# Layer 3 attention: TensorE's steps written out, two sets of key parts, value products in one piece

## The reference, cut to what matters

```python
q = q_input @ W_Q + b_Q                     # 16 x 56 x 128, as 16 heads of 8
k = kv_input @ W_K + b_K                    # 16 x 1500 x 128
v = kv_input @ W_V + b_V
sim = jnp.einsum('bhqd,bhkd->bhqk', q, k) / jnp.sqrt(jnp.float32(D_H))
sim = jnp.where(mask, neg_inf, sim)
attn = jax.nn.softmax(sim, axis=-1)
out = jnp.einsum('bhqk,bhkd->bhqd', attn, v)
...
return out @ W_O + b_O
```

## Time and profile before

| | us |
|---|---|
| Median of 3 runs | 1829.14 (1823.56 to 1829.15) |
| The profiled execution | 1828.54 |
| Its span | 1826.8 |
| PE busy in the span | 1546.7 (85%) |
| DVE busy | 1257.7 (69%) |
| ACT busy | 834.4 (46%) |
| POOL busy | 321.7 (18%) |

### The profile page before, as it was taken

How to read it: one execution, slowest core, us unless ns; L and a number is a source line. 1 busy time by engine, 2 the same in 40 slices (tenths; PEclk the granted TensorE clock), 3 DMA queues, 4 the chain that set the end, 5 groups by cost and what they waited for, 6 DMA issues and landing times. The chain is left out here.

```text
span 1826.8 us, 40229 instructions
## 1 busy us (share of the span) xinstructions
PE 1546.7 (85%) x15246; PEld 1295.7 (71%) x15246; DVE 1257.7 (69%) x2561; ACT 834.4 (46%) x1241; POOL 321.7 (18%) x437
## 2 busy tenths in 40 slices
PE   3897397456899999999999995679898889897895
PEld 2896276336799999999999982346676667675795
DVE  4313653685788888888888873367676768785698
ACT  1332132133566666666666640335454445453332
POOL 0110000001323343323343300030000000000230
PEclk8898698667999999999999998789999999999898
DMA  2112598000211111111111000153544354450210
GB/s 40 40 35 72 125 228 195 25 9 1 68 35 35 35 36 58 40 34 34 34 36 59 6 0 6 29 139 88 121 97 111 91 118 110 99 116 8 70 36 22
DMA packets 93087, 116.02 MB, mean 64 GB/s; under 512 B 12337, under 2 KB 78306, under 8 KB 92962
## 3 DMA queue, kind: packets, MB, share of 16 engines
q1 hardware_dynamic: 92962, 114.19, 24.8%
HBM read 76.35 MB, written 0.46 MB: 42 GB/s over the span
## 5 line engine op out<-in xcount | busy, mean ns | idle before, releaser
L2306 DVE TENSOR_REDUCE l3att_parts<-PS 112x1 f32<-112x500 f32 x384 | 244.3, 671 | 104.3 <-PE PS L2049 103.3
L1728 ACT CAST l2att_PT<-PS 125x512 fp32r<-125x512 f32 x336 | 175.2, 594 | 221.1 <-PE PS L1667 221.1
L1768 DVE TENSOR_REDUCE l2att_neg<-PS 128x1 f32<-128x1500 f32 x112 | 192.7, 1721 | 77.6 <-PE PS L1660 77.6
L1774 DVE TENSOR_TENSOR l2att_PT<-PS,l2att_PT 125x512 fp32r<-125x512 f32 x336 | 210.2, 681 | 1.5 <-ACT l2att_PT L1728 1.5
L2049 PE MATMUL PS<-l3att_KS,l3att_QB 97*112 97x500 f32 x384 | 169.0, 492 | 47.0 <-issue 24.2
L2180 ACT ACTIVATE l3att_P<-PS 125x1344 f32<-125x1344 f32 x128 | 165.3, 1291 | 77.4 <-PE PS L2068 77.4
L1667 PEld LDWEIGHTS PS<-all_ident,l_P 128*125 128x125 f32 x1344 | 163.5, 187 | 14.6 <-DVE l_P L1782 6.0
L1737 ACT ACTIVATE l_P<-PS,l2att_neg 128x1500 f32<-128x1500 f32 x112 | 171.2, 1529 | 5.0 <-DVE l2att_neg L1768 5.0
L1699 PE MATMUL PS<-l2att_PT,l_cc 125*128 125x256 f32 x576 | 170.5, 296 | 0.0
L1667 PE MATMUL PS<-all_ident,l_P 128*125 128x128 f32 x1344 | 165.4, 273 | 4.3 <-DVE l_P L1782 4.3
L1701 PE MATMUL PS<-l2att_PT,l_cc 125*128 125x256 f32 x576 | 162.5, 282 | 0.0
(11 more groups left out here) (518 smaller groups left out, 2960.1 us busy)
## 6 DMA issues: line engine op xcount, KB each, us to landing
l3att_KS<-l3att_kh SPq DMA_DIRECT2D x128, 187.5 KB, 4.3
l_QP<-in_ctxT SPq DMA_DIRECT2D x8, 1500.0 KB, 11.5
l_cT<-in_ctxT SPq DMA_DIRECT2D x16, 750.0 KB
l_c<-in_ctx SPq DMA_DIRECT2D x16, 750.0 KB
l3att_cT<-in_ctxT SPq DMA_DIRECT2D x16, 750.0 KB, 4.5
l3att_KS<-l3att_kl SPq DMA_DIRECT2D x64, 187.5 KB, 4.4
l_QP<-in_ctx SPq DMA_DIRECT2D x8, 1344.0 KB
l0f_w<-in_L_ffn_W SPq DMA_DIRECT2D x16, 256.0 KB, 3.1
```

What stands on the lines that cost most here:

```text
L1728: act.copy(PT[:, 4 * g:4 * g + 4, PLACE[u1], 0, :], PS[0:CHUNK, 3 * s1 + g, :].rearrange("k (c r) -> k c r", r=128)).then_inc(hi_in, 1)
L1768: v.tensor_reduce(neg[:, s:s + 1], E, XY_AXES, ALU.max, negate=True).then_inc(top_in, 1)
L1774: v.tensor_tensor(PT[:, 4 * g:4 * g + 4, at, 1, :], PS[0:CHUNK, 3 * s1 + g, :].rearrange("k (c r) -> k c r", r=128), PT[:, 4 * g:4 * g + 4 ...
L2306: v.tensor_reduce(parts[:, u % 2, half, i:i + 1], PS[0:HROWS, PLACES[p], 0:BANK_KEYS], X_AXIS, ALU.max, negate=True).then_inc(top_in, 1)
```

## The change

Three edits, all in `attend_sets`:

- PE's steps 0 to 68 are all written out; ACT, DVE and POOL keep their loops.
- `kh` and `kl` become two tiles each, taken in turn by the batch, and ACT's wait for the copies of the batch before is gone.
- In PE's step all 12 chunks of `values` come in one piece after `rows` 0 and 1, with a wait for both `powers` of step n-1. `rows` 2 moves behind the value projection, next to `rows` 3. Between `turned` 0 and `turned` 1 only `rows` 4 and 5 stay.

```diff
-            kh, kl = (self.sb(ctx, n, [128, KEYS], F32R) for n in ("kh", "kl"))
+            kh, kl = ([self.sb(ctx, f"{n}{s}", [128, KEYS], F32R) for s in range(2)] for n in ("kh", "kl"))
...
-                        for r, src, done in ((0, kh, kh_in), (1, kh, kh_in), (2, kl, kl_in)):
+                        for r, src, done in ((0, kh[s], kh_in), (1, kh[s], kh_in), (2, kl[s], kl_in)):
...
-                    def values(chunks):
+                    def values():
                         s, a = (u - 2) % UNROLL // SETS, (u - 2) % SETS
-                        if chunks[0] == 0:
-                            pe.wait_ge(m_in, n - 1)
-                            if known is None or known >= 4:
-                                pe.wait_ge(o_in, n - 3)
-                            pe.wait_ge(vh_in, (n - 2) // SETS * BANKS + BANKS)
-                            if known == 2:
-                                pe.wait_ge(blank, 1)
-                        for k in chunks:
-                            if k % PART == 0 or k == chunks[0]:
-                                pe.wait_ge(p_in, 2 * n - 3 + k // PART)
+                        pe.wait_ge(m_in, n - 1)
+                        if known is None or known >= 4:
+                            pe.wait_ge(o_in, n - 3)
+                        pe.wait_ge(vh_in, (n - 2) // SETS * BANKS + BANKS)
+                        pe.wait_ge(p_in, 2 * n - 2)
+                        if known == 2:
+                            pe.wait_ge(blank, 1)
+                        for k in range(CHUNKS):
...
                     if before:
-                        values((0, 1, 2, 3))
+                        values()
                     if then:
                         maxima()
...
-                    if now:
-                        rows((2,))
                     if late or g >= 2 and more:
...
                     if now:
-                        rows((3,))
+                        rows((2, 3))
                     if then:
                         turned(0)
                     if now:
                         rows((4, 5))
-                    if before:
-                        values((4, 5, 6, 7, 8, 9, 10, 11))
                     if then:
                         turned(1)
 
-                run_steps(pe, GROUPS, LAG, UNROLL, one, peeled=1)
+                for n in range(GROUPS + LAG):
+                    one(n, n % UNROLL, n)
...
-            def high_keys(act, b, i, bank):
+            def high_keys(act, b, s, i, bank):
                 act.wait_ge(k_ps, b * BANKS + i + 1)
-                act.activation(kh[:, BANK_KEYS * i:BANK_KEYS * i + BANK_KEYS], PS[:, bank, 0:BANK_KEYS],
+                act.activation(kh[s][:, BANK_KEYS * i:BANK_KEYS * i + BANK_KEYS], PS[:, bank, 0:BANK_KEYS],
...
                     if g < BANKS and more:
-                        if g == 0:
-                            for x in range(SETS):
-                                act.wait_ge(ks_in[u // SETS][x], n // UNROLL * 48 + 48)
-                        high_keys(act, b + 1, g, SIDE)
+                        high_keys(act, b + 1, 1 - u // SETS, g, SIDE)
...
-                        low_keys(b + 1, g, SIDE)
+                        low_keys(b + 1, 1 - u // SETS, g, SIDE)
```

More of the change, by code:

```diff
@@ L2097, in values @@
                                                start=k == 0, stop=k == CHUNKS - 1)
-                        if chunks[-1] == CHUNKS - 1:
-                            mm.then_inc(o_ps, 1)
+                        mm.then_inc(o_ps, 1)
                     now, then, before = live(known, 0, GROUPS), live(known, 1, GROUPS), live(known, 2, GROUPS)
@@ L2158, in _ @@
                 for i in range(BANKS):
-                    high_keys(act, 0, i, i)
+                    high_keys(act, 0, 0, i, i)
                 act.wait_ge(cleared, 1)
@@ L2260, in _, with low_keys @@
                 chain = Chain(v, step)
-                def low_keys(b, i, bank):
+                def low_keys(b, s, i, bank):
                     at = slice(BANK_KEYS * i, BANK_KEYS * i + BANK_KEYS)
                     v.wait_ge(kh_in, b * BANKS + i + 1)
-                    v.scalar_tensor_tensor(out=kl[:, at], in0=PS[:, bank, 0:BANK_KEYS], scalar=bk[:, 0:1],
-                                           in1=kh[:, at], op0=ALU.add, op1=ALU.subtract).then_inc(kl_in, 1)
+                    v.scalar_tensor_tensor(out=kl[s][:, at], in0=PS[:, bank, 0:BANK_KEYS], scalar=bk[:, 0:1],
+                                           in1=kh[s][:, at], op0=ALU.add, op1=ALU.subtract).then_inc(kl_in, 1)
                 layer_norm(v, chain, XN, X, ln, 1e-5, xn_ready)
@@ L2275, in _ @@
                 for i in range(BANKS):
-                    low_keys(0, i, i)
+                    low_keys(0, 0, i, i)
                 v.wait_ge(f_ps, 1)
```

## The result

Before, measured beside the change, takes 1826.35 us (4 runs, 1817.76 to 1829.15), the changed kernel 1963.57 (4 runs, 1962.69 to 1977.51): a ratio of 1.0771 with a 95% interval of 1.0741 to 1.08. Forecast were 1889 us, with a range of 1855 to 1925. The direction is right; the time is 75 us above the forecast and 39 above the range.

A forecast was written before the change was run, and what follows sets the result against it. PE's own work was taken to set the layer 3 step; 13 batches at +37.5 us, with +7, +5.5 and +3 for other steps, gave 1881.5, and +7.5 for clock falls gave 1889 us, range 1855 to 1925.

The forecast's parts named there:

- The two handoffs: PE's waits for ACT's exponential in every layer 3 step: 2.29 us before the value products, 2.27 before the second `turned`.
- Rivals 3: Handoffs to the exponential mostly covered, steps of 7.7 to 7.8 us, about 1856 us; chance 0.10.
- 4 (1780 to 1792): Faster: layer 3 steps stay bound by PE's own work, so the gains come through, 1780 to 1792 us; chance 0.04.
- The steps at full clock: Layer 3 attention steps of a batch: first 7.5 us, the other three 8.3 each, 32.4 a batch.
- the sum at full clock: Layer 3 attention's step changes, together +53 us on the profiled execution's 1828.54, giving 1881.5 us before any clock falls.
- The clock: PE's clock falls from new idle stretches in layer 3 steps: 5 falls, +7.5 us, bounds 0 and 33.
- Rival 1: PE's clock falls regularly, in one of three steps or more: 1915 us, up to 1940 with slower steps; chance 0.15.
- The loop written out: Writing out PE's layer 3 loop removes 24.2 us of issue waits; with cold stretches and long key waits, worth 35.9.
- Straight code itself costs nothing visible: In PE's written-out layer 3 code, steady steps take the same 6.67 us.
- Two sets: Two sets of key parts remove a stall in each batch's first step, worth about 1 us a batch.
- DVE's and ACT's loop turns: Loops kept on these engines in layer 3: 0.6 us a turn, hidden by DVE's idle time; upper bound 25 us.

The follow-up runs named there:

- the order alone: The kernel before with only the new order of PE's step, in the loop, with one set of key parts: 1941.75 us, ratio 1.063.
- The filled kernel: The changed kernel with unused identity products, four before the value products' wait and three before the second `turned`: 1887.71 us, ratio 1.0339.
- half of the wait: The changed kernel with value chunks 0 to 5 waiting only for the first exponential, the rest for the second: 1865.73 us, ratio 1.0208.
- the kernel written out alone: The kernel before with only PE's steps written out, old order and one set of key parts: 1801.62 us, ratio 0.988.

## Why the prediction was wrong, point by point

**The two handoffs: right.** 2.39 and 2.19 us for 2.29 and 2.27, and PE's waits for the exponential are 83.7 us, just under the 90 to 110 named. Two lengths, read from three places of the stage's end, gave the handoffs of nearly every step. Rivals 3 (1856) and 4 (1780 to 1792) fall with it.

**The steps at full clock: nearly right, off in two that partly cancel.** The second and third step take 8.25 and 8.3 (8.3). The first takes 6.6 in the order alone, where 7.5 was forecast: without the key wait and with one projection it loses more than half of 1.46. The fourth takes 8.7 with a warm clock, not 8.3; the 1.08 us wait for the reciprocal is paid in full, not in half. 6.6 + 8.25 + 8.3 + 8.7 = 31.9 us a batch, for 32.4, so 6.5 us less in 13 batches. The filled kernel as a whole (1882.4 without its issue stalls) meets the 1881.5 by errors that cancel; a batch of it takes 425.8 / 13 = 32.75 us; take away what the fillers themselves cost, (32.75 - 31.9) x 13 = 11 us, and the sum at full clock was about 10 us too high.

**The clock: the failed step.** I took "5 falls, +7.5", with 22 falls and +33 as the upper bound. Measured are 33 steps under 0.95 and 61 us or more. This term alone carries the time out of the range: 1889 + 53.5 is 1942.5. I put the step by the rows of the stage's end, where idle stretches of 0.68, 0.47 and 0.67 left the clock up. But there are only three of them, at the end, and the longer of the two new stretches is 1.01 us in the kernel after, not 0.8 to 0.9. Nor is one length a limit by itself: in step 12 of the kernel before, a stretch of 1.26 us left the clock up, and 1.30 us in step 20 brought it down. And I had written down the right worry, two stretches close together whose sum, 1.7, is above the 1.30 that brought the clock down in the row, and then went by each length by itself. Rival 1 names the mechanism, at a chance of 0.15, and its price was also too low: at one fall in three steps and 1.5 us for each. The clock is down in nearly two of three steps, and 61 us over 33 is 1.85 us for each. What decides which steps fall is not shown: steps with the same stretches (37 and 38) do either.

By the rule of the Trainium skill that I had weighed (TensorE: Matmul & The Clock Gate, "Why this matters for your kernels") gaps near 1 us would leave the clock up. The runs do not agree: the clock is 0.84 through the stage and the filled kernel, with more work, is 76 us faster. The measurement decides.

**The loop written out: right for the old order, wrong for this one.** "Straight code itself costs nothing visible" holds in 52 of 52 steps where the products lie between other work, and there the gain was 22 to 28 us. In the new order 13 stalls of 20.6 us came back: a second term put at nothing, on steps of the old order. They need both: straight code (in the loop only the turns stall) and the new order (none in the old). A reading that fits is that PE, released from a wait, runs 96 short products and their weight loads in 1.4 us, faster than instructions arrive, while in the old order the same instructions are spread. Shown is that each stall ends just behind the landing of a block of instructions, and that three blocks of 13 set off late, behind key copies; that the burst is what makes the other ten late is argued. Against the simple form of it stands that most stalls fall in steps 19 to 31 of 69, though every step has the burst. Also, the kernel with fillers has only 5.3 us of them, the one with half of the wait 18.4.

By the Trainium skill (Runtime: NRT & Kernel Launch, "Instruction fetch mechanics") straight code is fetched ahead. The 52 steps of the old order agree with it (0 us of stalls). Here 10 of the 13 blocks behind a stall did set off ahead, yet too late, so being fetched ahead didn't hide the 20.6 us.

**Two sets: right, and somewhat more than I gave.** -18 us alone, -24 beside straight code. In the new order next to nothing (medians of -8 in the loop, +5 written out).

**DVE's and ACT's loop turns: right.** They cost PE nothing; DVE's own issue wait is 1.7 us in 5 times.

**How the errors add up.** 1889 forecast; +53.5 for the clock (61 in place of 7.5) and +20.6 for stalls in straight code make 1963.1, for 1963.6 measured. This closes by its making, as the 61 are what the filled kernel left over; it tests nothing. Two other ways to the clock's cost: PE is busy 396.9 us with the matmuls of the 52 steps, and 331.0 in the kernel written out alone, at clock 1.00, so 66 more; and 501.9 less 20.6 of stalls less 13 warm batches of 31.9 leaves 67. So the clock is worth 61 to some 70 us, and about 10 us of that is made up by the sum at full clock, which was too high.

**What stays open.** What makes the blocks of instructions late where no copy is in their way, and why only in some of the steps. Why two steps with the same idle stretches differ in their clock. And why the clock of the same kernel is lower in one execution than in another (0.84 and 0.88) with the same idle stretches.

## What to carry to other kernels

A wait placed where the engine has other work ahead of it cost nothing here, and the same wait placed first cost its whole length and, with another near it, the clock; before merging two blocks of products into one piece, look at what each of their waits had ahead of it. Look at the idle stretches of a step together when judging the clock, not at each by itself, and test with a filler: if useless products in the gaps make the kernel faster, at least that much of the loss was clock. A sum that closes on terms taken from the same measurement proves nothing; get each term a second way. Take a change with several parts as several changes: two of the three here gain 46 us together, and the third then loses 186.

## What the runs showed of the hardware

- Idle stretches of some 0.4 to 0.7 us and 1.0 us in a step of 8.3 us brought TensorE's clock from 2.4 to 1.2 GHz in 28 of 52 steps (the order alone) and in 33 (the change); some of these stand beside loop turns or issue stalls. With either filled it was down in 3 and 5 steps, all beside other waits or stalls. The same stretches left the clock up in the rest of the steps.
- Seven unused 128x128 products a step (about 1.9 us of PE's time, mostly in its gaps) kept the clock at 1.00 and gained 76 us.
- A loop of PE with some 1976 to 2104 instructions stalled 3 to 5 us at every turn, and its instructions were transferred again each time (63 and 57 blocks of 16384 bytes in 52 steps); one with some 1336 did neither (10 blocks).
- Straight code stalled PE up to 4.1 us at once, at nearly the same places of the program in two executions. Each of the 13 stalls ended 1.3 to 1.7 us after a block of instructions had landed; the three longest came with the DMA engines 89 to 100% busy.
